# GNN layer and mixture-of-experts layer on one core: group sums computed already turned, with each routing and copying step moved within the turn

## What is computed

```
msgs = layernorm(x)[src] * edge_weight[:, None]
agg  = segment_sum(msgs, dst, num_segments=12500)
x    = x + agg @ W.T + b
xn   = layernorm(x)
probs = softmax(xn @ gate_w + gate_b);  top2 of 8, weights not renormalised
x    = x + sum over the two chosen experts e of  prob_e * (gelu(xn @ W1[e] + b1[e]) @ W2[e] + b2[e])
```

## Time and profile before

| | us |
|---|---|
| median of 3 runs (2973.94 to 2983.93) | 2977.66 |
| profiled execution, its device time | 2972.63 |
| its span in the trace | 2970.9 |
| POOL busy | 1830.6 |
| PE busy | 2196.5 |
| DVE busy | 1502.6 |
| ACT busy | 685.0 |
| mean granted TensorE clock | 0.869 |

### The profile page before, as it was taken

One profiled execution on the slowest core, in us unless ns is written; L12 is line 12 of the kernel. 1 busy time (PEld: TensorE's weight loads), 2 busy tenths in 40 slices (PEclk: granted clock), 3 DMA queues, 4 the chain that ended last, 5 costly groups with the idle time before them and its releaser, 6 DMA issues.

```text
span 2970.9 us, 47965 instructions
## 1 busy us (share of the span) xinstructions
PE 2196.5 (74%) x11446; PEld 1714.3 (58%) x11447; DVE 1502.6 (51%) x6264; ACT 685.0 (23%) x1950; POOL 1830.6 (62%) x1912
## 2 busy tenths in 40 slices
PE   3666767877777889787787786897887687665585
PEld 2444444665565677565665565676666566554474
DVE  8865454354363554554554544545555363554122
ACT  3411111221221222221221222222222222222131
POOL 6666777767767667767677677675765655500121
PEclk8778879888898999898898898998998888886798
DMA  9654747658568578578698587595976867655674
GB/s 344 231 191 140 234 119 239 212 179 261 193 191 256 189 237 292 173 250 278 198 293 260 167 273 228 181 299 164 297 256 206 262 214 251 180 177 152 208 242 159
DMA packets 306367, 659.36 MB, mean 222 GB/s; under 512 B 61604, under 2 KB 198598, under 8 KB 290342
## 3 DMA queue, kind: packets, MB, share of 16 engines
q1 hardware_dynamic: 213686, 402.45, 41.1%
q0 software_dynamic: 90960, 248.50, 27.6%
q10 hardware_dynamic: 1440, 5.26, 0.5%
HBM read 552.90 MB, written 212.26 MB: 258 GB/s over the span
## 4 chain that ended last, share of the span: by engine, by line
PE 30%; DVE 16%; SPq 16%; POOL 14%; issue 12%; DMA 11%; ACT 1%; DVEq 0%; ACTq 0%; POOLq 0%
POOL rows L383 13%; PE bank L648 9%; SPq L511 9%; PE bank L728 7%; PE bank L741 7%; DMA slots<-stage 4%; SPq L348 3%; DMA w<-in_w 2%; PE bank L680 2%; DVE spread L1037 2%; DMA results<-y_sb,result_i 1%; PE bank L671 1%; DVE item_t L1210 1%; DMA xi<-slots 1%; PE bank L718 1%
## 5 line engine op out<-in xcount | busy, mean ns | idle before, releaser
L383 POOL DMA_INDIRECT rows<-xhat,src_t x1536 | 1476.3, 961 | 522.3 <-issue 460.3
L648 PE MATMUL bank<-rows,spread 128*80 128x256 f32 x3328 | 878.7, 424 | 152.8 <-issue 63.7
L648 PEld LDWEIGHTS bank<-rows,spread 128*80 128x80 f32 x3328 | 552.1, 170 | 423.5 <-issue 197.7
L410 POOL DMA_INDIRECT results<-y_sb,result_i x231 | 229.1, 992 | 520.7 <-DVE y_sb L1243 477.1
L728 PE MATMUL bank<-xiT,w 128*128 128x128 f32 x3696 | 479.2, 285 | 66.0 <-issue 39.0
L728 PEld LDWEIGHTS bank<-xiT,w 128*128 128x128 f32 x3696 | 462.1, 199 | 98.6 <-issue 52.9
L741 PE MATMUL bank<-w,hT 128*128 x1848 | 480.4, 406 | 14.9 <-issue 7.5
L1050 DVE TENSOR_TENSOR acc<-acc,bank 128x160 f32 x208 | 67.0, 322 | 669.9 <-PE bank L638 639.5
L741 PEld LDWEIGHTS bank<-w,hT 128*128 128x128 f32 x1848 | 361.5, 205 | 72.4 <-issue 24.8
L879 ACT ACTIVATE hT<-bank,b1T 128x128 f32<-128x128 f32 x924 | 264.3, 368 | 575.8 <-PE bank L728 572.4
L1037 DVE TENSOR_SCALAR spread<-iota_w,dst_rel,wgt 128x80 f32<-128x80 f32 x1536 | 379.3, 339 | 0.1
(11 more groups left out here) (170 smaller groups left out, 1720.1 us busy)
## 6 DMA issues: line engine op xcount, KB each, us to landing
w<-in_w SPq DMA_DIRECT2D x231, 512.0 KB
slots<-stage SPq DMA_DIRECT2D x784, 136.0 KB
xi<-slots SPq DMA_DIRECT2D x231, 136.0 KB, 4.0
stage<-sorted_x SPq DMA_DIRECT2D x98, 272.0 KB
got<-results SPq DMA_DIRECT2D x97, 256.0 KB
rows<-xhat,src_t POOLq DMA_INDIRECT x1536
x_t<-in_x SPq DMA_DIRECT2D x97, 128.0 KB, 3.1
x_d<-x_t SPq DMA_DIRECT2D x97, 128.0 KB
```

What stands on the lines that cost most here:

```text
L383: pool.indirect_dma_start(rows[q][:, c, :], None, x if g < RAW else xhat, bass.IndirectOffsetOnAxis(ap=src_t[:, g * CG + c:g * CG + c + 1] ...
L410: pool.indirect_dma_start(results, bass.IndirectOffsetOnAxis(ap=result_i[i % 2][:], axis=0), y_sb[i % 2][:], None).then_inc(y_out[i % 2], 16)
L648: done = nc.tensor.matmul(B_SUM[0:W, 0:D], spread[g % 2][:, c, :], rows[q][:, c, :], start=c == 0, stop=c == CG - 1)
```

## The change

**Sums.** Now the gathered rows are stationary and spread moves: for each half k of the 256 features, eight matmuls with 128 x 128 weights and 80 moving columns, straight into the turned form. There are two banks for it, used in turn. `copy_sums` and `turn_sums` are gone, and add_group adds from the bank. In the first 16 groups the means are added in the same way, 16 matmuls with one column of minus8 broadcast to 128 x 128.

```
 def sums(g):
-    if g:
-        pe.wait_ge(sums_n_ready, g)
-    for c in range(CG):
-        done = nc.tensor.matmul(B_SUM[0:W, 0:D], spread[g % 2][:, c, :], rows[q][:, c, :], ...)
+    if g >= 2:
+        pe.wait_ge(added, g - 1)
+    for k in range(KD):
+        to = B_SUM[g % 2][:, k * W:(k + 1) * W]
+        for c in range(CG):
+            done = nc.tensor.matmul(to, rows[q][:, c, k * P:(k + 1) * P], spread[g % 2][:, c, :], ...)
+        if g < RAW:
+            for c in range(CG):
+                done = nc.tensor.matmul(to, minus8[:, c:c + 1].to_broadcast([P, P]), spread[g % 2][:, c, :], ...)
```

```
-            elif k not in soft_at and gate_at.get(end, tau) < tau:
+            elif k not in soft_at and gate_at.get(end, tau + 1) <= tau:
...
-            t.results = [s[0] for s in turns[-1].steps if s[0] >= 0]
-            t.combines = turns[-1].fetches
+            t.combines, t.stores = turns[-1].fetches, turns[-1].combines
...
+        for back in turns if not busy else turns[:-1]:
+            t.results += [s[0] for s in back.steps if s[0] >= 0 and s[0] not in result_at]
```

```
+                    for u in t.stores:
+                        store_out(u)
                     for step in t.steps:
                         if step[3] >= 0:
                             load_xi(step[3])
-                    for u in t.combines:
-                        store_out(u)
                     for u in t.fetches:
                         load_results(u, u in EPOCH_TILES)
-                    if t.linear >= 0:
-                        store_x1(t.linear)
+                    if t.load_x >= 0:
+                        load_x(t.load_x)
...
+                    if t.stage >= 0:
+                        copy_runs(t.stage)
```

More of the change, by code:

```diff
@@ L174, in plan @@
                 t.choose = k
-            elif k not in soft_at and gate_at.get(end, tau) < tau:
+            elif k not in soft_at and gate_at.get(end, tau + 1) <= tau:
                 soft_at[k] = tau
                 t.softmax = k
[L178 to L181, removed]
+        if send_next < NT and place_at.get(PART_OF[send_next], tau) < tau:
+            t.mask = t.sort = send_next
             send_next += 1
-        if t.runs >= 0 and t.runs == PARTS[PART_OF[t.runs]][1] - 1:
-            sent_at[PART_OF[t.runs]] = tau
+        if turns and turns[-1].sort >= 0:
+            t.stage = turns[-1].sort
+            if t.stage == PARTS[PART_OF[t.stage]][1] - 1:
+                sent_at[PART_OF[t.stage]] = tau
         open_to = max([sure_items(k) for k in sent_at if sent_at[k] < tau], default=0)
@@ L756, in turns @@
                             up(b)
-                    if t.add >= 0:
-                        turn_sums(t.add)
+                    if t.gate >= 0:
+                        turn_node(t.gate)
+                    if t.linear >= 0:
+                        linear(t.linear, fast)
+                    for a, _, c, _ in t.steps[:1]:
+                        step_down(a, c)
+                    if t.gate >= 0:
+                        logits(t.gate)
+                    if t.place >= 0:
+                        rank(t.place)
                     if t.sort >= 0:
                         sort(t.sort, 0)
-                    if t.gate >= 0:
-                        turn_node(t.gate)
-                    for a, _, c, _ in t.steps[:1]:
-                        step_down(a, c)
+                    if t.sums >= 0:
+                        sums(t.sums)
                     if t.sort >= 0:
                         sort(t.sort, 1)
-                        n_sorted[0] = t.sort + 1
-                    if t.linear >= 0:
-                        linear(t.linear, fast)
-                    if t.gate >= 0:
-                        logits(t.gate)
-                    if t.choose >= 0:
-                        rank(t.choose)
-                    if t.sums >= 0:
-                        sums(t.sums)
                     for a, b, c, _ in t.steps[1:]:
@@ L884, in turns @@
                 for t in plan:
[L885 to L886 removed]
+                    if t.stage >= 0:
+                        copy_sorted(t.stage, 1)
+                        store_sorted(t.stage)
                     if 0 <= t.sums < RAW:
```

172 lines of the change are left out of this document (69 added, 103 removed).

## The result

The changed kernel takes 2821.12 us (median of 4 runs, 2813.22 to 2827.19) beside 2979.89 us of the kernel before (median of 4): a ratio of 0.9467, 95% interval 0.9438 to 0.9497. Forecast were 2765, range 2665 to 2895. The sign and the range held; 56 us of the gain did not come.

The account below looks back on a forecast made before the run. POOL's queue was taken as the bound: 3 + 2335 us of its work + 125 of waits put the gathers' end at 2463; a 297 tail made 2760 of span, forecast 2765 us, range 2665 to 2895.

Parts of the forecast that it names:

- The first 16 groups, +20: Head: means as 32 more matmul records on PE cost +1.2 us a group, +20 us in all, bounds 0 and +70.
- Rival B: Slower: PE's clock stays at its lower level; 15.4 us a turn and 3500 us if all PE is low; chance 0.06.
- 32 records of sums, 3.6 us: PE's sums per group: 32 records of 80 columns take 3.6 us against 3.62 before, bounds 2.1 and 4.2.
- Gathers behind the head, -142: From group 16's first gather to the last gather's end: -122 for the gathers' end less +20 for the head.
- the scatter now stands a turn later: POOL's queue: the later scatter leaves the y_sb wait only as DVE's delay, 15 us kept of 166.
- Behind the last gather, -88: Tail after the last gather: 385 us before, pieces summing to -93 (tail 292), taken as 297.
- (1): Tail: the last sums end 15 us behind the last gather instead of 35, -20 us.
- (2): Tail's one-step turns: eight at 12.5 us, 100 us instead of 178, plus one three-step turn of 13.4: -64.
- (3): Tail's three-step turns: PE is the bound, and one bank for `up` costs nothing.
- (4): Last scatter to the end, 27 us: six buffers instead of two let fetch, add and store overlap, -9 us.
- A: POOL waits for sums about as long as for y_sb before: waits 210, tail 340, about 2890 us; chance 0.19.
- C: Moved steps fail: SP's staging wait holds loads or ACT stands before staging, POOL's waits return; 2940 to 2985 us; chance 0.05.

Follow-up runs that it names:

- e5: Changed kernel with each result scattered one turn after its last step instead of two, four buffers kept: 2819 us, 0.946 of the kernel before, quiet chip.
- e7: Changed kernel with results scattered one turn after their last step and two y_sb buffers instead of four: 3650 us, 0.960 of the kernel before, slow chip.

## Why the prediction was right, and where it was wrong

- **The first 16 groups, +20: wrong, the step that failed.** Measured +65.7 us. I took 0.11 to 0.12 us a record, the high level, and kept 0.214 as the upper bound (64 records, 13.7 us). The upper bound is what happened: 13.7 us in the group shown, 0.214 a record. The old side of the sum was wrong as well. It took 3.6 + 1.4 = 5.0 us for the sums and means of a group, the high level, but the kernel before has 7.0 us in its head:

```profile
104.03 5.99 PE L648 MATMUL bank<-rows,spread 128*80 128x256 f32 x16 [1.74 <-issue]
```

So PE's share grew by 6.7 us a group and not by 2.3. The clock of 0.81 hid this, since it counts the first 48 us, before the first recorded change, as 1.00; from 48 to 220 us it is 0.76. Rival B's mechanism, the low level, is what came, in a part of the kernel and not in the whole; its remark that with the sums alone low a turn has "no slack but not slower" fits groups 20 to 79.
- **32 records of sums, 3.6 us: right by size** (3.69 at the high level), **wrong as "no gain and no loss".** With the old sums the groups from 20 on take 34 us less on the quiet chip. At the low level 32 records take 7.12 us, and turns in which PE has stood show the loss; the 60 groups with the clock at 0.76 for 0.89 lose 3 us. The Trainium skill ("TensorE: Matmul & The Clock Gate", LDWEIGHTS) gives an estimate of 3.4 us for these loads, and the trace agrees at the high level with 3.69. The rule on row groups in Part 3 of the same page of the Trainium skill, by which it would be 5.6, does not hold here.
- **Gathers behind the head, -142: the number is right (-141.9) by luck.** It is -186.7 for the reordering and +44.8 for the new sums, two misses of the same size. The last gather ends at 2509 us where 2463 was forecast; that miss is the head's. PE's waits for mask and `both`, 39.4 us together, were forecast under 60, and y_sb under 40: 1.8. But "the scatter now stands a turn later" had no part in it (e5), and the ring of four has none shown (e7). PE stands less, and that is the likely place of the 187 us, but its moved steps, softmax, rank and the queues were not tried one by one. For the sums 60 us were forecast and 61.7 came; with the old sums it is 25.3.
- **Behind the last gather, -88 taken: -75; two misses partly cancel.** (1) The last sums end at 2530.3, 21 us behind the last gather, for 15. (2) From there to the first scatter at the pitch of three steps, 2659.0, it is 129 us for the 100 forecast; the same stretch before was 185 (2620.0 to 2805.2). So 56 us were saved for the 78 forecast, the second term that was off by more than 20. (3) Then come 32 scatters 4.49 us apart in 138.3 us, as before in 138.6, with the clock at 1.00; the 13.4 us for one more turn of three steps are not there. (4) From the last scatter to the end it is 22.3 us for 18. With the old sums the tail is 309.4, so none of the saving was the sums'.
- **Rivals.** A (one wait takes another's place) did not come at its price of 210, but one sign of being wrong was met: POOL waits 171.3 us for sums in all, over the 150 named, 109.6 of them for the sums of the first 16 groups, which A did not have in mind. e5 shows A's mechanism. C did not come: SP waits 76.8 us for `staged`, under the 100 named. But the queues' gain is less than the prediction made of it. SP no longer waits for x_t (476.6), and now stands 625.1 us in front of the load of the next x_t until the one stored from ACT's queue has landed (121.0 before), ahead of copy_runs in its order. What that costs was not tried.

```profile
SPq L476 <- DMA x_d<-x_t: 625.1, 48, 33.1
```

- The sum: 46 us too little for the head and 13 too much off the tail give the 59 us of span between forecast and measured.

## To carry to other kernels

A change of two parts should be priced in two parts: here one was worth 264 us and the other cost 112, and the total looked like a success of both. Before taking copies and turnings off two engines, ask whether anyone waits for them. Before making TensorE's records narrower and more numerous, find out by a run of that shape which clock level they will run at. Where it is low, a few unused columns in each record can be the cheapest remedy (shown here on slow chips, 0.941 for 0.959 and, with the old sums, 0.963). A lower clock costs only where somebody waits for the engine: look for those turns and not at the mean. Where a queue has two waits for the same engine, removing one can move it into the other.

## What the runs showed of the hardware

- **The head ran at the low level with PE in work 209.62 of 232 us, and wider records lifted it for nothing.** 64 records a group of 128 x 128 weights and 80 columns ran at 0.214 us each. With 128 columns in each the same number of records cost no more, and most ran at the high level (190 ns a load for 333).
- **A lower granted clock alone cost 3 us in 60 groups** (657.2 us at 0.76, 654.6 at 0.89), where POOL's gathers set the pace.
- **The recorded clock before its first change** reads 1.00 in a stretch whose records have the low level's pace: 48 to 280 us of the slow chip's changed kernel, with 421 ns a matmul of the means.

```profile
48.00:280.00 232.00, 209.63 (x941) 202.41 (x942) 130.64 (x636) 52.53 (x116) 105.04 (x111) 1.00 0.49 170
...
L633 PE MATMUL bank<-spread,minus 128*128 128x80 f32 x512 | 115.5, 420 | 0.0
```

- **The same program takes 28% longer on some chips** (before 3819 us for 2978). POOL's gathers are as long as ever (946 ns). PE's stream breaks in the middle of a group's matmuls, with nothing waited for: 341.1 us in front of the sums, 59.8 on the quiet chip. ACT stands so too, 216.6 us in front of gelu for 15.6. Changed kernel, slow chip, PE's timeline, then waits:

```profile
1502.44 2.44 PE L629 MATMUL bank<-spread,rows 128*128 128x80 f32 x20
1505.84 0.23 PE L629 MATMUL bank<-spread,rows 128*128 128x80 f32 x1 [0.96 <-issue]
1506.58 0.23 PE L629 MATMUL bank<-spread,rows 128*128 128x80 f32 x1 [0.51 <-issue]
1507.97 2.12 PE L629 MATMUL bank<-spread,rows 128*128 128x80 f32 x10 [1.16 <-issue]
```

```profile
PE bank L629 <- issue: 341.1, 278, 5.5
ACT hT L850 <- issue: 216.6, 57, 11.9
PE bank L703 <- issue: 120.7, 120, 7.4
```

The cause was not tried. In the head PE is busy for 209.63 us of 232 against 209.62 on the quiet chip, so the engine itself is not slower there. That instructions reach the engines late would fit, and no run shows it.
